# Second attention of a fused four-block kernel: output product, routing and row transfers of a chunk placed nearer behind its tiles

## The reference, cut to what matters

```python
# block 3: attention over fixed offsets (0 to 32, 48, 64, 96, 128, 192), 16 heads of 8
scores = einsum("bhnd,bhond->bhno", q, K_all) * scale + pos_bias      # K_all: k at each offset back
alpha  = softmax(scores, axis=-1)
out    = einsum("bhno,bhond->bhnd", alpha, V_all)
gate   = sigmoid(x @ Wgate.T + bgate)
block3 = flat * gate @ Wout.T + bout
# block 4: two experts of eight for each row (of a second layer norm xn of its input)
abel   = gelu(xn @ abel_w + abel_b)
logits = xn @ moe_gate_w + moe_gate_b
topw, topi = top_k(logits, 2)                                         # weights: softmax of the two
moe    = sum over the two experts e of w_e * (gelu(xn @ ew1[e] + eb1[e]) @ ew2[e] + eb2[e])
moe    = moe @ expm(g0) @ expm(g1) @ expm(g2)
g      = sigmoid([abel, moe] @ gc_w + gc_b)
block4 = residual + abel * (1 - g) + moe * g
```

## Time and profile before

| | us |
|---|---|
| median of 3 runs | 1568.72 (1564.0 to 1570.36) |
| profiled execution | 1564.88 |
| its span, first to last instruction | 1562.8 |
| granted TensorE clock, mean | 0.882 |

### The profile page before, as it was taken

One profiled execution on the slowest core, in us unless ns is written; L12 is line 12 of the kernel. 1 busy time (PEld: TensorE's weight loads), 2 busy tenths in 40 slices (PEclk: granted clock), 3 DMA queues, 4 the chain that ended last, 5 costly groups with the idle time before them and its releaser, 6 DMA issues.

```text
span 1562.8 us, 37817 instructions
## 1 busy us (share of the span) xinstructions
PE 1287.3 (82%) x13524; PEld 879.8 (56%) x13524; DVE 1165.2 (75%) x3833; ACT 745.7 (48%) x1523; POOL 715.8 (46%) x1043
## 2 busy tenths in 40 slices
PE   4598889988899888999987799598898988548880
PEld 2344544445454454444446799477777767447770
DVE  5588697887988869889766565478999888834445
ACT  1055555555555455555555455154554433116653
POOL 3023142332433324324223554477887887645554
PEclk9699999999999999999998899778877676559995
DMA  4655627555274561745731311031111111212225
GB/s 117 107 94 93 103 31 121 79 92 94 32 125 77 89 101 26 126 74 93 121 158 35 100 43 28 25 84 44 44 44 46 50 50 40 101 61 79 84 77 167
DMA packets 73881, 123.21 MB, mean 79 GB/s; under 512 B 17534, under 2 KB 46083, under 8 KB 72800
## 3 DMA queue, kind: packets, MB, share of 16 engines
q1 hardware_dynamic: 64472, 105.26, 35.4%
q0 software_dynamic: 7616, 13.59, 2.6%
q10 hardware_dynamic: 1608, 1.95, 0.6%
HBM read 30.40 MB, written 17.60 MB: 31 GB/s over the span
## 4 chain that ended last, share of the span: by engine, by line
PE 43%; DVE 31%; issue 12%; POOL 6%; ACT 4%; DMA 3%; SPq 1%; DVEq 0%; another core or an unknown queue 0%; ACTq 0%; POOLq 0%
DVE first L833 6%; PE A L632 5%; PE S L615 4%; PE S L1099 4%; DVE S L836 4%; PE S L604 4%; PE A L2108 3%; PE S L2101 2%; PE S L1659 2%; DVE tA L812 2%; DVE tB L813 2%; PE A L1106 2%; PE A L1670 2%; PE S L596 2%; DMA Qp<-mT 2%
## 5 line engine op out<-in xcount | busy, mean ns | idle before, releaser
L717 ACT ACTIVATE P<-S 128x512 f32<-128x512 f32 (+3 forms) x768 | 333.4, 491 | 283.4 <-PE S L615 274.7
L907 POOL TENSOR_SCALAR_AFFINE_SELECT P<-P 128x256 f32<-128x256 f32 (+1 forms) x256 | 116.9, 460 | 388.4 <-ACT P L717 388.1
L615 PE MATMUL S<-Qp,Kp 121*128 121x512 f32 (+3 forms) x768 | 252.5, 393 | 37.8 <-DVE tB L813 11.2
L604 PE MATMUL S<-Kp,Qp 120*128 120x512 f32 (+3 forms) x768 | 252.3, 398 | 32.5 <-DMA Kp<-big 15.8
L836 DVE CUSTOM_DVE_ANT_0 S<-S,later 128x512 f32<-128x512 f32 (+3 forms) x512 | 239.0, 513 | 43.8 <-PE S L604 37.1
L604 PEld LDWEIGHTS S<-Kp,Qp 120*128 120x128 f32 x768 | 133.8, 196 | 165.6 <-issue 75.0
L615 PEld LDWEIGHTS S<-Qp,Kp 121*128 121x128 f32 x768 | 139.2, 192 | 115.8 <-issue 24.4
L833 DVE TENSOR_REDUCE first<-S 128x1 f32<-128x512 f32 x256 | 164.3, 683 | 48.4 <-PE S L604 48.2
L632 PE MATMUL A<-P,V 128*9 128x512 f32 (+3 forms) x1536 | 174.9, 503 | 5.4 <-POOL P L907 5.3
L2245 POOL DMA_INDIRECT yq<-yq,id x71 | 69.5, 979 | 70.9 <-DVE yq L2208 44.7
L1892 POOL TENSOR_TENSOR prod<-mid,kT 128x128 f32<-128x128 f32 x160 | 72.8, 488 | 41.4 <-ACT mid L1727 31.6
(11 more groups left out here) (356 smaller groups left out, 2687.7 us busy)
## 6 DMA issues: line engine op xcount, KB each, us to landing
Qp<-big SPq DMA_DIRECT2D x63, 256.0 KB
Kp<-big SPq DMA_DIRECT2D x62, 256.0 KB
Qp<-big SPq DMA_DIRECT2D x63, 128.0 KB
Kp<-big SPq DMA_DIRECT2D x62, 128.0 KB
xq<-xq SPq DMA_DIRECT2D x71, 72.0 KB
yb<-yq SPq DMA_DIRECT2D x8, 528.0 KB, 7.1
big<-in_w SPq DMA_DIRECT2D x4, 1024.0 KB, 9.6
big<-vt SPq DMA_DIRECT2D x32, 128.0 KB
```

Source lines behind the costliest of these rows:

```text
L604: te.matmul(S[s][:, 512 * h:512 * h + n], Q[0:120, h, 128 * qt:128 * qt + 128], K[0:120, h, 512 * part:512 * part + n], start=True, stop=T ...
L615: te.matmul(S[s][:, 512 * h + c:512 * h + 512], K[0:121, h, 128 * kb:128 * kb + 128], Q[0:121, h, 512 * qh + c:512 * qh + 512], start=True ...
L717: se.activation(k.P[(w.n - 1) % NP0][:, h, c:512], S[s][:, 512 * h + c:512 * h + 512], ACT.Exp, scale=SCALE0).then_inc(p.done("st").h, 1)
L907: ge.affine_select(P[:, :, start:c + 128], P[:, :, start:c + 128], [[0, 2], [1, wide]], ALU.is_ge, 0.0, base=start - c, channel_multiplier ...
```

## The change

The four items of the output product are placed at other keys of `PLACES`: `aT1` at (0, 1), `ga` at (1, 0), `wo1` at (1, 1), `xo` at (2, 0) with two chunks' distance, where they stood at (2, 2), (3, 0), (3, 2) and, three chunks behind, (0, 0). The routing of chunk c starts at t = 4c + 10 in place of 4c + 12, `nT` to `pos` follow one another at shorter distances, and the sends stand at three spots of a tile in place of two. Behind the last tile more routing is added in the third stage, and the head of the fourth stage's list is written anew for what is left.

```diff
-PLACES = {(0, 0): (("xo", -3), ("vw", 0, 0), ("bo", 1)), (0, 2): (("xT1", 1),),
-          (1, 0): (("k1", 1, 0), ("gate", 0)), (1, 2): (("vw", 0, 1),),
-          (2, 0): (("k1", 1, 1),), (2, 1): (("qg", 1),), (2, 2): (("aT1", -2), ("ln1", 2), ("ln2", 2)),
-          (3, 0): (("rstd", 2), ("ga", -2), ("gg", 1), ("qm", 1, 0)), (3, 1): (("vt", 1),), (3, 2): (("qm", 1, 1), ("wo1", -2), ("ln3", 2))}
-STEPS1 = [("q1", 0, 2), ("p1", 1, 0), ("q2", 1, 2), ("p2", 2, 0), ("q3", 2, 2), ("copy", 3, 0), ("nT", 4, 2), ("lg1", 5, 2), ("top", 6, 0), ("rank", 6, 2),
-          ("pos", 7, 0)]
-SENDS1 = [(7, 2), (8, 0), (8, 2), (9, 0), (9, 2), (10, 0), (10, 2), (11, 0)]
+PLACES = {(0, 0): (("vw", 0, 0), ("bo", 1)), (0, 1): (("aT1", -2),), (0, 2): (("xT1", 1),),
+          (1, 0): (("ga", -2), ("k1", 1, 0), ("gate", 0)), (1, 1): (("wo1", -2),), (1, 2): (("vw", 0, 1),),
+          (2, 0): (("xo", -2), ("k1", 1, 1)), (2, 1): (("qg", 1),), (2, 2): (("ln1", 2), ("ln2", 2)),
+          (3, 0): (("rstd", 2), ("gg", 1), ("qm", 1, 0)), (3, 1): (("vt", 1),), (3, 2): (("qm", 1, 1), ("ln3", 2))}
+LATE1 = 10
+STEPS1 = [("q1", 0, 2), ("p1", 1, 0), ("q2", 1, 2), ("p2", 2, 0), ("q3", 2, 2), ("copy", 3, 0), ("nT", 3, 0), ("lg1", 4, 0), ("top", 4, 2), ("rank", 5, 0),
+          ("pos", 5, 2)]
+SENDS1 = [(6, 0), (6, 1), (6, 2), (7, 0), (7, 1), (7, 2), (8, 0), (8, 1)]
...
         def routing(t, spot):
-            for late in range(2, -1, -1):
-                c = t // 4 - 3 - late
-                if 0 <= c < NCH:
-                    for name, more in steps.get((t % 4 + 4 * late, spot), ()):
-                        self.route.add(o, name, c, *more, ring="X" if name in R1PE else None, banks=X)
+            for c in range(NCH):
+                for name, more in steps.get((t - 4 * c - LATE1, spot), ()):
+                    self.route.add(o, name, c, *more, ring="X" if name in R1PE else None, banks=X)
...
-        for name, c in (("xo", NCH - 2), ("aT1", NCH - 1), ("ga", NCH - 1), ("wo1", NCH - 1), ("xo", NCH - 1)):
-            piece(name, c)
+        c = NCH - 1
+        piece("aT1", c)
+        self.route.add(o, "p2", c - 1)
+        for n in range(4):
+            self.route.add(o, "send", c - 2, n // 4, n % 4)
+        piece("ga", c)
+        self.route.add(o, "q3", c - 1)
+        self.route.add(o, "copy", c - 1)
+        piece("wo1", c)
+        piece("xo", c)
...
-        c = NC1 - 4
-        send(c, 2)
-        routing(c + 2, "q1", "p1")
-        routing(c + 1, "nT", "lg1")
...
-        routing(c + 3, "rank", "pos")
-        o.add("tiles")
-        send(c + 2, 8)
-        send(c + 3, 8)
+        c = NC1 - 1
+        routing(c, "q1", "p1")
+        routing(c - 1, "nT", "lg1")
+        send(c - 2, 6)
+        routing(c, "q2", "p2")
+        routing(c - 1, "top", "rank")
+        routing(c, "q3", "copy")
+        routing(c - 1, "pos")
+        send(c - 2, 8)
+        routing(c, "nT", "lg1", "top", "rank")
         o.add("ab", 0, ring="S")
+        o.add("ab", 1, ring="S")
+        routing(c, "pos")
+        o.add("tiles")
+        send(c - 1, 8)
+        send(c, 8)
         o.add("ab", 2, ring="S")
         o.add("ab", 3, ring="S")
         o.add("ab", 4, ring="S")
         for f in range(4):
             o.add("fold", f, ring="S")
```

More of the change, by code:

```diff
@@ L1973, in send @@
                 r.add(o, "send", c, n // 4, n % 4)
-        c = NC1 - 4
-        send(c, 2)
-        routing(c + 2, "q1", "p1")
-        routing(c + 1, "nT", "lg1")
-        send(c, 4)
-        routing(c + 2, "q2", "p2")
-        routing(c + 1, "top")
+        c = NC1 - 1
[8 more added lines that the diff above has]
+        routing(c, "nT", "lg1", "top", "rank")
         o.add("ab", 0, ring="S")
-        routing(c + 1, "rank")
-        routing(c + 2, "q3", "copy")
-        routing(c + 1, "pos")
+        o.add("ab", 1, ring="S")
+        routing(c, "pos")
+        o.add("tiles")
+        send(c - 1, 8)
         send(c, 8)
[L1987 to L1992, removed]
-        o.add("ab", 2, ring="S")
[L1994 to L1998, removed]
-        routing(c + 3, "top")
+        o.add("ab", 2, ring="S")
         o.add("ab", 3, ring="S")
-        routing(c + 3, "rank", "pos")
-        o.add("tiles")
-        send(c + 2, 8)
-        send(c + 3, 8)
         o.add("ab", 4, ring="S")
```

## The result

| | before | after |
|---|---|---|
| median | 1566.36 (1559.04 to 1570.36) | 1587.72 (1582.36 to 1592.47) |
| profiled span | 1562.8 | 1581.5 |

The changed kernel is slower: ratio 1.0131, 95% interval 1.0101 to 1.0161. Two later groups of runs gave 1.0162 (1.0101 to 1.0223) and 1.0155 (1.0117 to 1.0194). The forecast was 1566.8 with a range up to 1580. What came is the mechanism of the slower rival, and the loop lost more than that rival's price.

The account below looks back on a forecast made before the run. VectorE, TensorE and GpSimd are nearly full in the attention loop, and GpSimd's transfers bound the last stage's head. +7 + 0 - 8.9 = -1.9 us on the 1568.72 median gives 1566.8; own range 1560 to 1574, widened to 1556 to 1580.

Parts of the forecast that it names:

- slower rival: Attention loop: VectorE waits for lg1 in each chunk's third tile; +11 us in all, 1579.7, chance 0.22.
- Term A: Attention loop up to the last L1820: added VectorE work, partly absorbed, plus waits; +7 us, between 0 and +20.
- 3.6 absorbed + 3 for waits and blocked applies: Attention loop: 3.6 us of 7.6 added VectorE work vanishes in idle time, 3 us comes on top.
- Rival 2: Attention loop's third tiles: five VectorE waits for lg1, 16.6 us in all; decides if 12 survive; 1579.7, chance 0.22.
- bound of +20: Attention loop's upper limit: 7.6 us of added work plus 12 us of surviving waits for lg1.
- the two near pairs: Attention loop: top follows lg1, and pos follows rank, inside one tile; one example gave a 3.9 us wait for lg1.
- Blocked applies: Attention loop: transfers lengthen VectorE's applies (L1395), 0.3 us for each transfer, 2 us for seven more.
- Term B: From the last L1820 to the stage boundary: added work and filled waits balance; 0 us, between -3 and +5.
- Term C: Head of the last stage, boundary to first expert transpose: fewer transfers, folds last; -8.9 us, between -11.7 and -5.

Follow-up runs that it names:

- s_before: The kernel before, unchanged, run again beside three others for a profile on one chip: 1566.95 us, loop 228.7.
- e1_places_only: Kernel before with only the output product's new places, routing and transfers as late as before: 1579.3 us, ratio 1.009 to the kernel before.
- e5_tile_apart: Changed kernel with lg1 and top, rank and pos a tile's start apart, same 20 transfers behind: 1524.09 us against 1530.42, ratio 0.9971.
- s_tile_apart: The kernel of e5_tile_apart, unchanged, run in a later group beside the kernel before: 1572.4 us, ratio 1.004.
- e9_pos_before_drain: e5_tile_apart with pos of the sixth chunk in the loop's last tile and its four transfers around p2: 1572.72 us, ratio 1.0048 to the kernel before.
- r_after_again: The changed kernel, unchanged, run again beside the kernel before: ratio 1.0162, loop 263.0 us.
- r_before_again: The kernel before, unchanged, run again for a profile in the same group: 1566.4 us, loop 230.6.

## Why the prediction was wrong, by its steps

- **Term A, the step that failed.** The forecast was +7, between 0 and +20; measured is +35.0. The first part was 7.6 of added work, and busy time grew by 7.4 (8.6 and 13.1 in the later pairs), with some time held inside instructions in it. The second part was "3.6 absorbed + 3 for waits and blocked applies", of which 2 were for the applies and so 1 for the waits. Nothing was absorbed, and idle time grew by 27.6. The waits for lg1 alone are 19.2. Rival 2 had read 16.6 off the rows of before for the same five places, 0.8 to 6 us each; measured are five of 2.0 to 4.9. So the number stood in the prediction, and the forecast set about 1 in its place, with the argument that TensorE bounds those tiles and isn't held. It was held: it waited 16.8 us for L1827 in place of 5.1, once behind each of the five waits for lg1 (13.3 us) and once ahead of the first (3.6, at tile 11).
- **The bound of +20 was no bound.** It was 12 us of the rival's waits plus the work. With all of them it is 7.6 + 16.6 = 24.2, and 35.0 came. The runs split the rest in another group, where the loss is 36.9: 22.2 go with the two near pairs, about their own waits, and 14.6 stay when they are gone, 5.7 as busy time and 9.0 as idle time, with the wait for av the largest (12.8 us; 2.0 in s_before). For TensorE being late with av the prediction had no term. Slots of ring X, of which it had no row either, cost e1_places_only 11.7 us, and the changed kernel none.
- **Blocked applies.** They were priced at 2 us for seven more transfers. In the last twelve tiles' stretch L1395 from x took 0.97 us before and 0.44 after, while a transfer took 1.15 before and 1.26 after. But over the whole loop other lines grew, L1395 from n from 0.38 to 0.51 us and the four scalings of mid (L1812 before, L1819 after) from 0.75 to 1.59. So no term can be read off one line. All lines together grew by 7.4, 0.2 less than the forecast had for work alone, so in this pair of profiles the holding took no more than before. The Trainium skill ("SBUF — State Buffer", section "SBUF: two separate sides") says that the ports which VectorE and GpSimd share are an exclusive lock, taken for a whole instruction, and that the other engine fully blocks. By the lines together, the full 0.67 us for each more transfer did not come on top here.
- **Term B.** 0 forecast, between -3 and +5. The prediction ended it where the boundary opens: 33.6 us behind the last L1827 (1347.90 to 1381.53) against 28.5, so +5.1, just past the bound. The boundary was said to be 2.7 us later than VectorE would let it, and opened 6.2 us behind the last xo. The last transfer was issued at 1376.86, 4.67 us ahead of the opening, and the same 4.67 stand in e5_tile_apart, s_tile_apart and e9_pos_before_drain. I take them for the transfer's landing, which the term had left out; the landing itself no view shows. e9_pos_before_drain, with the last transfers sooner, opened 1.8 us sooner than e5_tile_apart.
- **Term C.** -8.9 forecast, between -11.7 and -5. From the boundary, as the prediction cut it, it is 39.9 us (1381.53 to 1421.41) against 57.8: -17.9, far past the bound. The order of ends was right: transfers, pad blocks, folds, transpose, TensorE without a gap. The last pos ended 24.0 us behind the boundary (22.8 forecast). The sizes behind it were wrong: the tile arithmetic ended 5.7 us behind pos where 10.5 had been carried over from before, a length with VectorE's waits in it; ab 2 was through TensorE ahead of the last pos, so the first fold waited only for its addition and started 30.6 us behind the boundary, not 37; and the folds took 8.5 us, not 10.3.
- **Luck.** Cut at the last xo, as in the section on the result, the two are -0.9 and -11.9, together -12.8 where -8.9 was forecast. That this sum is near is partly luck: B was 5.1 too low and C 9.0 too high.
- **Sum.** 35.0 - 0.9 - 11.9 + 0.3 = 22.5 with what lies behind the transpose; the profiled span grew by 18.7, since tile 8 came 3.7 us sooner in it.

What stays open: why TensorE was granted 0.70 to 0.73 in the changed loop, and 0.74 to 0.78 with the steps apart and 0.74 to 0.79 before. It was busy for 230.0 us with 5526 matmuls, where before 5366 took 207.1. In the middle group the changed loop was 32.4 us longer at a clock of 0.73 against 0.74 (r_after_again, r_before_again), so a lower clock is not what the loss takes. No run tells whether the lockstep lowers the clock or both have another cause, nor how much of the last 9 us of idle time in s_tile_apart is the clock's doing. Not tried were own PSUM space for lg1 and rank, and the order of s_tile_apart with fewer transfers in the loop, which would tell what the transfers have in the 14.6 us.

No version beats the kernel before where that takes 1567 us. s_tile_apart beats the changed kernel (1572.4 against 1591.97 in one group). The same file, as e5_tile_apart, beat the kernel before only in the group at 1530, and by 0.3%.

## What to carry to other kernels

When a step is moved nearer to its producer, read off the rows when the producer will be through in its own queue, and if that gives a sum of waits, put that sum in the forecast: here the waits of the near pairs added up to 19.7 us and setting the pairs apart gave 22.2. That the other engine is the bound takes nothing off it, since in a loop where two engines take turns at being late, a wait of one comes back as a wait of the other. A busy time may hold waits of its own, so compare it instruction by instruction before calling it work. Before any item is moved in a list with shared slots, list which item each one takes its slot from and when that is given back: a wait for an unrelated item looks like contention and is only order. And an engine's transfers are not over when it has issued them: here the boundary opened 4.67 us behind the start of the last issue.

## What was not expected of the hardware

- A barrier stayed closed well behind GpSimd's last issue. In e5_tile_apart the last transfer was issued 0.9 us behind the last xo and the boundary opened at 5.5; from issue to opening it is 4.67 us there, in the changed kernel and in e9_pos_before_drain. That this is the transfers' landing is inferred.
- The same file took 1524 us in one group of runs and 1572 in another (the kernel before 1530 and 1567). From the first expert transpose to the last it was 100.0 us in e5_tile_apart and 117.1 in s_tile_apart, at nearly the same granted clock (1.00 and 0.99), for the same work; windows of the one and the other:

```profile
1377.71:1477.69 99.98, 88.91 (x624) 76.17 (x623) 54.83 (x302) 74.78 (x210) 62.61 (x64) 1.00 0.35 94
```

```profile
1405.36:1522.46 117.10, 94.36 (x622) 78.08 (x623) 54.98 (x299) 70.70 (x206) 62.27 (x64) 0.99 0.29 81
```

  The attention loop took 227.6 and 243.3; tiles 18, 22, 26 and 30 hold the difference (16.4 us), with 7.0 to 8.1 us each there and 10.9 to 12.7 here. So one order was 0.3% faster than the kernel before in one group and 0.4% slower in the other; what sets the two apart no run shows, and both groups have the same chip number on record.
- Pad blocks issued while transfers ran took 1.3 us each in the changed kernel (10.74 for eight), where in the kernel before three took 12.69.
